# Two biases, one softmax sum and a block scaling written in another form, in a two-layer decoder kernel

## The chip, the cores and the metric

One core of a Trainium2 chip runs the whole program. The metric is the device time of one execution in microseconds. Engines are TensorE (PE, with its weight loads as PEld), VectorE (DVE), ScalarE (ACT), GpSimd (POOL) and SyncE (SP), which issues the DMAs. Each runs its own list of instructions in order, and they meet in semaphores.

## The reference

The input x is 8 items of 256 tokens by 512, with a context of 8 x 256 x 128. Two layers follow each other, each of three residual steps, every one on the layer norm of x:

```
layer 0   x += softmax(mask(q k' / sqrt(32))) v @ Wo.T + bo     16 heads of 32, causal;
                q = x Wq.T + bq, k = x Wk.T + bk, v = x Wv.T + bv
          x += softmax(q k' / 4) v      32 query heads of 16 on the context, 8 key heads, no mask
          x += mx(silu(mx(x, w_gate)) * mx(x, w_up), w_down)    512 -> 2048 -> 512
layer 1   x += ((scan + x Dp) * sigmoid(x Wg + bg)) @ Wo        h = exp(d A) h + d d, along the tokens
          x += causal attention of x on keys and values expanded from the context, 16 heads of 32
          x += x W.T + low-rank experts, 2 of 8 per token
```

`mx` rounds both operands in blocks of 32: a block is divided by a power of two taken from its largest absolute value, rounded to a few bits, and multiplied back.

## The kernel before, in words

`build` writes the instructions of every engine. Each stage is a class with one generator per engine, and each `yield` ends a piece. `TURNS0` holds, per engine, a long string of letters; `side_by_side` advances the generator that the next letter names. So the order on each engine is fixed, and the stages of neighbouring items are interleaved: in layer 0 the masked attention (`attn`, banks 0 to 2), the attention on the context (`mix`, banks 3 to 5), the rounding of the weights (`quantised`) and the hidden layer (`ffn`, banks 6 and 7); in layer 1 the scan (`ssm`), the attention on the context (`cross`) and the experts (`lora`). The program's item loop runs over 8 items, each with two blocks of 128 tokens (TT = 2) and four chunks of 128 features (DC = 4).

**Products.** Where fp32 exactness is wanted, an operand is a pair of fp16 tiles, high and low. `product` (its matmul stands on L200) makes three matmuls per pair. `Loader` brings a weight to a staging tile by DMA, copies it to the high half on ACT (L285) and subtracts on VectorE to get the low half (L292).

**`Attention`** is used twice, as `attn` and as `cross`. Per item: transpose the normed rows (L422), q and k for four chunks (L200, and for `attn` L431), v for two token blocks (L200), row maxima of the scores (L481 to L495 on TensorE, L679 and L683 on VectorE), then for each of 16 heads the transposed scores (L522, L523), an exponential on ACT into `p` (L642), and the causal mask on POOL (L737). A head's `p` is 128 x 384: first the key block 0 for all 256 queries, then key block 1 for queries 128 to 255. For every four heads, L534 makes the values' product in a column-tiled form (four matmuls side by side on 32 columns of the array each), and L542 the sums over keys. L542 keeps one row for each head and each query block, 32 rows of 128 columns for all 16 heads: `ones_of_four[:, 2c+t, :]` picks the row, and the three blocks of `p` are three matmuls of 128 columns per head. L692 takes the reciprocal of the 128 x 128 sums, L557 spreads it back over the features of a head (16 matmuls of 128 columns for each of two halves), L698 multiplies, L705 splits, and the output product (L200) follows; L719 adds it to x.

**The biases.** The value bias `bv` is not added to v, since the weights of a softmax sum to 1. Instead `bv @ Wo.T` is made once, with item 0's output product (12 matmuls on L200), added to x of item 0 (L713) and to the output bias `bo` (L715), which POOL adds to x for every item. The gate bias of the scan stage enters its bank by one matmul per token block (L1385), whose stationary `two_rows` has ones in row 0 and row 64, with the bias's high half in the upper and its low half in the lower rows of `g_b`.

**The rounding.** `dve_quantise` takes the blocks' maxima (L1133), clamps them (L1135), keeps the exponent as `e` (L1137), makes the inverse `inv` (L1139) and multiplies (L1142); `dve_rounded` clamps and multiplies back with `e` (L1148, L1150). It runs 5 times an item. `e` is larger than the block's scale by a constant factor; the factors WEIGHT, ROWS and GATE are carried through the products and taken out in the `Tanh` scale and, as DOWN, in the last addition to x (L1279, L1283). The 12 units of weights do the same (L794 to L822).

**Banks.** `Banks.take` makes TensorE wait until a PSUM bank has been read. Of several banks that wait on the same semaphore it issues one wait, with the larger value.

## Time and profile before

| | |
|---|---|
| time, median of 3 runs | 1603.94 us (1602.54, 1603.94, 1609.94) |
| the profiled execution: time, span | 1603.94 us, 1602.2 us |
| busy: TensorE, VectorE, ScalarE, GpSimd | 85%, 83%, 65%, 27% of the span |
| mean granted TensorE clock | 0.939 of full speed |
| last quantisation of layer 0, first gate bias of layer 1 | at 972 us, at 856 us (the layers overlap) |

The span runs from the first to the last instruction of the profile; the time holds the launch around it as well. Busy time is a sum over stages with different limits. The chain of work that ended last is followed back from the last instruction, at each step to what released it or to the instruction before it on its engine. A matmul on fp32 data appears as two records, and its length in the trace includes the way through the array, so that neighbours overlap; what a stream of them costs is read from start to start.

### The profile page before, as it was taken

How to read it: one execution, taken by the hardware profiler on the slowest of the kernel's cores; microseconds unless marked ns; L12 is line 12 of the kernel's file. 1: busy time of each engine (PE TensorE's matmuls, PEld its weight loads, DVE VectorE, ACT ScalarE, POOL GpSimd, SP SyncE). 2: the span in 40 equal slices, each digit the busy share in tenths (PEclk: the TensorE clock that was granted, in tenths of full speed). 3: DMA queues.
4: the chain of work that ended last, by engine and by line, in shares of the span. 5: the costliest groups of instructions: out<-in, count | busy, mean ns of one | idle time of the engine just before them, and what ended most of it. 6: DMA issues, size and time to landing. Idle time of an engine off the chain costs nothing.

```text
span 1602.2 us, 32850 instructions
## 1 busy us (share of the span) xinstructions
PE 1361.3 (85%) x13068; PEld 745.7 (47%) x13068; DVE 1332.5 (83%) x1965; ACT 1037.2 (65%) x1884; POOL 428.2 (27%) x495
## 2 busy tenths in 40 slices
PE   3778878879899999898978767879999998999986
PEld 2454535344445453444443333446555555555643
DVE  6988989979879888887798899888788888978743
ACT  3244365465673865765695769886899788989431
POOL 1432141132240422321331240241222313122310
PEclk9697989799999999999999988889999999999988
DMA  6313122200201111002120003011020211101020
GB/s 223 93 54 93 34 68 68 74 15 1 75 15 41 36 41 42 21 22 54 63 89 28 1 1 132 20 41 44 2 71 13 59 39 33 41 5 44 2 81 27
DMA packets 54201, 76.24 MB, mean 48 GB/s; under 512 B 8480, under 2 KB 23840, under 8 KB 53536
## 3 DMA queue, kind: packets, MB, share of 16 engines
q1 hardware_dynamic: 54048, 74.14, 16.2%
q8 instruction: 104, 1.70, 0.4%
q14 instruction: 49, 0.40, 0.1%
HBM read 38.98 MB, written 9.44 MB: 30 GB/s over the span
## 4 chain that ended last, share of the span: by engine, by line
PE 47%; DVE 29%; ACT 10%; issue 7%; POOL 4%; DMA 1%; SPq 1%; ACTq 0%; DVEq 0%; POOLq 0%
PE bank L200 16%; DVE mix_NM L1079 4%; PE bank L1178 4%; PE bank L534 3%; DVE ssm_HS L1537 2%; PE bank L542 2%; PE bank L522 2%; PE bank L992 2%; PE bank L1204 2%; PE bank L557 2%; DVE ffn_m L1133 2%; PE bank L977 2%; POOL attn_P L737 2%; PE bank L495 1%; DVE ffn_Z L1142 1%
## 5 line engine op out<-in xcount | busy, mean ns | idle before, releaser
L1052 ACT ACTIVATE mix_P<-bank 128x512 f32<-128x512 f32 x256 | 142.3, 604 | 50.6 <-PE bank L977 50.2
L1079 DVE TENSOR_REDUCE mix_NM<-bank 128x2 f32<-128x512 f32 x256 | 162.8, 682 | 11.2 <-PE bank L952 10.4
L737 POOL TENSOR_SCALAR_AFFINE_SELECT cross_P<-cross_P 128x256 f32<-128x256 f32 x128 | 90.5, 717 | 272.9 <-ACT cross_P L642 272.4
L1296 POOL TENSOR_TENSOR ffn_room<-ffn_room 128x512 f32<-128x512 f32 x64 | 89.9, 1406 | 263.9 <-ACT ffn_room L1235 167.0
L1537 DVE TENSOR_TENSOR_SCAN ssm_HS<-ssm_DA,ssm_DD 128x1024 f32<-128x1024 f32 x64 | 150.3, 2348 | 10.1 <-ACT ssm_DD L1488 5.5
L737 POOL TENSOR_SCALAR_AFFINE_SELECT attn_P<-attn_P 128x256 f32<-128x256 f32 x128 | 89.6, 713 | 243.7 <-ACT attn_P L642 243.7
L1485 ACT ACTIVATE ssm_DA<-ssm_Z,A_T 128x255 f32<-128x255 f32 x256 | 110.9, 498 | 3.1 <-DVE ssm_HS L1537 2.7
L642 ACT ACTIVATE attn_P<-bank 128x384 f32<-128x384 f32 x128 | 63.8, 498 | 63.1 <-PE bank L523 62.7
L642 ACT ACTIVATE cross_P<-bank 128x384 f32<-128x384 f32 x128 | 62.6, 489 | 50.9 <-PE bank L523 50.5
L1543 DVE TENSOR_TENSOR ssm_HS<-ssm_HS,ssm_CS 128x1024 f32<-128x1024 f32 x64 | 82.0, 1281 | 0.9
L1460 ACT ACTIVATE ssm_Z<-bank 128x512 f32<-128x512 f32 x128 | 72.2, 599 | 13.4 <-PE bank L1374 12.8
L1178 PE MATMUL bank<-gate,ffn_XQ 128*128 128x512 bf16 x256 | 68.8, 392 | 13.0 <-DVE ffn_room L1260 12.7
L992 PE MATMUL bank<-mix_P,mix_V 128*32 128x256 f32 x1024 | 69.6, 395 | 2.8 <-DVE mix_XN L1095 2.2
L1178 PE MATMUL bank<-up,ffn_XQ 128*128 128x512 bf16 x256 | 68.5, 392 | 0.5 <-ACT ffn_room L1235 0.5
L977 PE MATMUL bank<-mix_Q,mix_K 64*128 64x256 f16 x512 | 53.2, 288 | 18.3 <-ACT mix_P L1052 15.6
L1488 ACT ACTIVATE ssm_DD<-ssm_Z 128x1024 f32<-128x1024 f32 x64 | 67.2, 1050 | 0.0
L952 PE MATMUL bank<-mix_K,mix_Q 64*128 64x256 f16 x512 | 51.6, 281 | 16.6 <-DVE mix_NM L1079 15.1
L1204 PE MATMUL bank<-down,ffn_room 128*128 128x512 bf16 x256 | 64.9, 389 | 0.0
L1231 ACT ACTIVATE ffn_room<-bank 128x512 f32<-128x512 f32 x64 | 38.9, 607 | 34.3 <-PE bank L1178 34.1
L1260 DVE SCALAR_TENSOR_TENSOR ffn_room<-ffn_room,bank 128x512 f32<-128x512 f32 x64 | 43.5, 680 | 19.3 <-ACT ffn_room L1231 19.3
L522 PE MATMUL bank<-attn_stack 128*128 128x256 f16 x128 | 39.1, 305 | 21.9 <-ACT attn_P L642 16.6
L1150 DVE TENSOR_TENSOR ffn_room<-ffn_room,ffn_e 128x1024 bf16<-128x1024 bf16 x40 | 54.3, 1357 | 1.4
(410 smaller groups left out, 4043.3 us busy)
## 6 DMA issues: line engine op xcount, KB each, us to landing
attn_stack<-attn_P SPq DMA_DIRECT2D x96, 128.0 KB, 2.4
cross_stack<-cross_P SPq DMA_DIRECT2D x96, 128.0 KB, 2.4
ffn_room<-f_gate SPq DMA_DIRECT2D x4, 1024.0 KB, 5.3
XR<-x SPq DMA_DIRECT2D x8, 512.0 KB, 6.8
ffn_room<-f_up SPq DMA_DIRECT2D x4, 1024.0 KB, 5.6
ffn_room<-f_down SPq DMA_DIRECT2D x4, 1024.0 KB, 4.9
x_mid<-XR SPq DMA_DIRECT2D x8, 512.0 KB, 3.0
XR<-x_mid SPq DMA_DIRECT2D x8, 512.0 KB, 3.7
```

The lines of the kernel that those rows point to most:

```text
L200: last = nc.tensor.matmul(out, a_, b_, start=(start and i == 0), stop=(stop and i == len(terms) - 1))
L642: nc.scalar.activation(self.p[h % 8][:, :], bank[self.b[0]][:, 0:S + P], ACT.Exp, scale=HD1 ** -0.5).then_inc(self.p_ready, 1)
L737: nc.gpsimd.affine_select(out=diagonal, in_=diagonal, compare_op=ALU.is_ge, fill=0.0, base=0, pattern=[[0, 2], [1, P]], channel_multiplier ...
L977: last = nc.tensor.matmul(bank[b4[i]][:, k * S:(k + 1) * S], self.k[rows, v // 2, k * P:(k + 1) * P], self.q[rows, v, :], start=(k == 0), ...
L992: last = nc.tensor.matmul(bank[b][32 * j:32 * j + 32, half * S:(half + 1) * S], self.v[:, k, g, :], self.p[(4 * g + j) % 8][:, k * S:(k + ...
L1052: nc.scalar.activation(self.p[h % 8], bank[b4[h % 2]][:, :], ACT.Exp, scale=HD2 ** -0.5).then_inc(s["p_ready"], 1)
L1079: nc.vector.tensor_reduce(self.nm[:, t, 16 * i + 2 * g:16 * i + 2 * g + 2], bank[b4[u % 3]][:, :].rearrange("p (c k) -> p c k", c=2), AX.X ...
L1178: last = nc.tensor.matmul(bank[b][:, :], self.xq[:, k, T * P:(T + 1) * P], w[:, k, fb * 512:(fb + 1) * 512], start=(k == 0), stop=(k == DC ...
L1204: last = nc.tensor.matmul(bank[b][:, :], self.iqt[:, f, :], self.down16[:, f, :], start=(f == 0), stop=(f == FC - 1))
L1296: nc.gpsimd.tensor_tensor(self.inter[q % 2][:, 512 * (g % 2):512 * (g % 2) + 512], self.sg[g % 2], self.up[g % 2], ALU.mult).then_inc(s["i ...
L1485: nc.scalar.activation(self.da[:, G % 2, k, 1:S], self.z[:, h, 1:S], ACT.Exp, scale=self.A_T[:, h:h + 1])
L1537: nc.vector.tensor_tensor_scan(flat(self.hs), flat(self.da), flat(self.dd), 0.0, ALU.mult, ALU.add).then_inc(s["hs_ready"], 1)
```

## The change

Six edits:

1. The sums of the softmax keep one row per head over 256 queries, in two matmuls per head (256 and 128 columns) in place of three of 128. The reciprocal covers 256 columns in place of 128, and the spreading has 8 matmuls of 256 columns per half in place of 16 of 128. Fewer columns of `ones_of_four` are set at the start.
2. `bv` is added to v by two matmuls of 512 columns (high and low half against the identity) per token block. The product `bv @ Wo.T`, its two additions and the wait of POOL go. The Loader brings `bv` broadcast to 128 x 512 in place of 128 x 4, and the first value product waits for the fourth load in place of the third.
3. The gate bias enters by two such matmuls in place of one; `two_rows` and its three memsets go, and the low half is made over 128 rows in place of 64.
4. `dve_quantise` and the weights' rounding make a further small tile `sc`, the block scale without the constant factor (`e` times 16, 8 or 0.25), and multiply back with it; the factors leave `Tanh`, L1279 and L1283, which become plain additions.
5. `Banks.take` issues one wait per bank.
6. The counts that TensorE waits for (`done_pool`, `made`) follow the smaller number of constants.

```diff
     def take(self, *banks):
-        last = {}
         for b in banks:
             if b in self.reader:
-                signal, value = self.reader.pop(b)
-                last[signal.num] = (signal, max(value, last.get(signal.num, (signal, value))[1]))
-        for signal, value in last.values():
-            self.engine.wait_ge(signal, value)
+                self.engine.wait_ge(*self.reader.pop(b))
...
-        ones_of_four = sb(top, "ones_of_four", [P, 2 * DC, 32])
+        ones_of_four = sb(top, "ones_of_four", [P, DC, 32])
...
                     if n == self.first and t == 0 and self.bv is not None:
-                        pe.wait_ge(*self.weights.ready(3))
+                        pe.wait_ge(*self.weights.ready(4))
                     banks.take(b)
+                    if self.bv is not None:
+                        for i, part in enumerate((self.bv.high, self.bv.low)):
+                            nc.tensor.matmul(bank[b][:, :], identh[:], part[:, :], start=(i == 0), stop=False)
...
-                        for i, t in enumerate((0, 1, 1)):
+                        for k, part, first in ((0, slice(0, S), 0), (1, slice(S, S + P), P)):
                             for j in range(4):
-                                last = nc.tensor.matmul(bank[sums][32 * j:32 * j + 32, 0:P], ones_of_four[:, 2 * c + t, :],
-                                                        self.p[(4 * c + j) % 8][:, i * P:(i + 1) * P],
-                                                        start=(c == 0 and i == 0), stop=(c == DC - 1 and i == 2))
+                                last = nc.tensor.matmul(bank[sums][32 * j:32 * j + 32, first:S], ones_of_four[:, c, :],
+                                                        self.p[(4 * c + j) % 8][:, part], start=(c == 0 and k == 0),
+                                                        stop=(c == DC - 1 and k == 1))
...
-                    for i in range(2 * TT):
+                    for i in range(2):
                         for j in range(4):
-                            at = 32 * j + 2 * TT * half + i
-                            last = nc.tensor.matmul(bank[b][32 * j:32 * j + 32, i * P:(i + 1) * P],
-                                                    ident[:, at:at + 1].broadcast_to([P, HD1]), self.rc[:, 0:P],
+                            at = 32 * j + 2 * half + i
+                            last = nc.tensor.matmul(bank[b][32 * j:32 * j + 32, i * S:(i + 1) * S],
+                                                    ident[:, at:at + 1].broadcast_to([P, HD1]), self.rc[:, :],
                                                     start=True, stop=True)
...
-                        if n == self.first and c == 2 and t == 0 and self.bv is not None:
-                            banks.take(self.b[1])
-                            product(bank[self.b[1]][:, :], [
-                                (self.bv.view(lambda t_: t_[:, k:k + 1].broadcast_to([P, P])),
-                                 self.wo.view(lambda t_: t_[:, k, :])) for k in range(DC)]).then_inc(self.vo_ps, 1)
-                            banks.read_by(self.b[1], self.vo_done, 2)
...
-                nc.vector.reciprocal(self.rc[:, 0:P], bank[self.b[2]][:, 0:P]).then_inc(self.r_ready, 1)
+                nc.vector.reciprocal(self.rc[:, :], bank[self.b[2]][:, 0:S]).then_inc(self.r_ready, 1)
...
-                    if self.bv is not None and n == self.first and t == 0:
-                        dve.wait_ge(self.vo_ps, 1)
-                        nc.vector.tensor_tensor(x[:, :, :], x[:, :, :], broadcast(bank[self.b[1]][:, :], 1, TT), ALU.add
-                                                ).then_inc(self.vo_done, 1)
-                        nc.vector.tensor_tensor(self.bo[:, :], self.bo[:, :], bank[self.b[1]][:, :], ALU.add
-                                                ).then_inc(self.vo_done, 1)
-                        dve.wait_ge(self.vo_done, 2)
...
-                    if n == 1:
-                        pool.wait_ge(self.vo_done, 2)
...
+                scaled = own(nc.vector.tensor_scalar(q_sc, q_e, 0.25, None, ALU.mult))
...
+                own.wait(scaled)
...
-                nc.vector.scalar_tensor_tensor(blocks(self.w16), blocks(y), -6.0, broadcast(q_e, 2, BLOCK), ALU.max,
+                nc.vector.scalar_tensor_tensor(blocks(self.w16), blocks(y), -6.0, broadcast(q_sc, 2, BLOCK), ALU.max,
...
+                own(nc.vector.tensor_scalar(sc, e, back, None, ALU.mult))
                 own.wait()
                 nc.vector.tensor_tensor(blocks(self.z8[:, :]), blocks(src), broadcast(inv, 2, BLOCK), ALU.mult,
...
-                        nc.scalar.activation(self.sg[g % 2], bank[b4[0]][:, :], ACT.Tanh, scale=GATE / 2
+                        nc.scalar.activation(self.sg[g % 2], bank[b4[0]][:, :], ACT.Tanh, scale=0.5
...
-                nc.vector.scalar_tensor_tensor(x[:, 1, :], bank[b4[1]][:, :], DOWN, x[:, 1, :], ALU.mult, ALU.add
+                nc.vector.tensor_tensor(x[:, 1, :], x[:, 1, :], bank[b4[1]][:, :], ALU.add
...
-                            nc.tensor.matmul(bank[b][:, :], two_rows[:], self.g_b[:, :], start=True, stop=False)
+                            for i, part in enumerate((self.g_b.high, self.g_b.low)):
+                                nc.tensor.matmul(bank[b][:, :], identh[:], part[:, :], start=(i == 0), stop=False)
...
-                               + [(whole(bv), A["bv"]), (whole(wo), chunk(A["Wo"]))],
+                               + [(whole(bv), A["bv"].partition_broadcast(P)), (whole(wo), chunk(A["Wo"]))],
```

## Rows read from the trace of the kernel before

**Rows 1.** The page's busy times and chain by engine; the cores' clock.

```profile
PE 1361.3 (85%) x13068; PEld 745.7 (47%) x13068; DVE 1332.5 (83%) x1965; ACT 1037.2 (65%) x1884; POOL 428.2 (27%) x495
...
PE 47%; DVE 29%; ACT 10%; issue 7%; POOL 4%; DMA 1%; SPq 1%; ACTq 0%; DVEq 0%; POOLq 0%
...
core 0: 1602.2 us, clock 0.939
```

**Rows 2.** The chain by line, 120 to 800 us, then 800 to 1602.

```profile
by line: PE bank L200 10.2%; DVE mix_NM L1079 7.4%; PE bank L1178 7.0%; issue 7.0%; PE bank L992 4.3%; POOL attn_P L737 3.5%; PE bank L977 3.3%; PE bank L952 3.2%; PE bank L1204 3.1%; DVE ffn_m L1133 2.4%; PE bank L534 2.4%; DVE ffn_room L1
...
by line: PE bank L200 23.2%; issue 7.0%; DVE ssm_HS L1537 4.9%; PE bank L534 2.9%; DVE ssm_HS L1543 2.4%; PE bank L542 2.4%; POOL cross_P L737 2.2%; PE bank L1402 2.2%; PE bank L1374 2.1%; PE bank L522 2.1%; DVE mix_NM L1079 2.1%; PE bank L
```

**Rows 3.** Busy time of L200 on TensorE (instructions), clock, DMA, by stretch.

```profile
120.00:800.00 680.00, 149.85 (x915) 0.95 0.16 44
800.00:1602.00 802.00, 317.31 (x2016) 0.94 0.14 39
```

**Rows 4.** Groups on VectorE: busy us, mean ns; idle before, releaser.

```profile
L1133 DVE TENSOR_REDUCE ffn_m<-ffn_room 128x32 f32<-128x1024 f32 x40 | 48.4, 1210 | 2.0 <-ACT ffn_room L357 1.6
...
L1093 DVE RECIPROCAL mix_RS<-bank 128x16 f32<-128x16 f32 x32 | 8.1, 253 | 24.6 <-PE bank L1007 24.5
...
L692 DVE RECIPROCAL attn_RC<-bank 128x128 f32<-128x128 f32 x8 | 7.6, 955 | 12.4 <-PE bank L542 12.4
```

**Rows 5.** Timeline of TensorE, 240 to 248 us: start, length, records.

```profile
241.13 0.86 PE L534 MATMUL bank<-attn_P,attn_V 128*32 128x256 f32 x16 [0.93 <-POOL attn_P L737]
241.80 0.84 PE L542 MATMUL bank<-attn_P,ones_of_four 128*32 128x128 f32 x24
242.46 1.05 PE L992 MATMUL bank<-mix_P,mix_V 128*32 128x256 f32 x16
...
245.01 0.39 PE L977 MATMUL bank<-mix_Q,mix_K 64*128 64x256 f16 x4 [0.18 <-ACT mix_P L1052]
245.33 1.07 PE L992 MATMUL bank<-mix_P,mix_V 128*32 128x256 f32 x16
246.22 1.93 PE L557 MATMUL bank<-attn_RC,ident 128*32 128x128 f32 x64
```

**Rows 6.** Timeline around the first and the last of 16 reciprocals.

```profile
92.11 0.96 DVE L692 RECIPROCAL attn_RC<-bank 128x128 f32<-128x128 f32 x1 [5.96 <-PE bank L542]
...
93.13 1.95 PE L557 MATMUL bank<-attn_RC,ident 128*32 128x128 f32 x64 [1.08 <-DVE attn_RC L692]
...
1559.26 0.96 DVE L692 RECIPROCAL cross_RC<-bank 128x128 f32<-128x128 f32 x1 [1.53 <-PE bank L542]
...
1560.54 1.73 PE L557 MATMUL bank<-cross_RC,ident 128*32 128x128 f32 x55
```

**Rows 7.** Timeline of VectorE at 109.6 us.

```profile
109.64 0.17 DVE L344 TENSOR_SCALAR mix_negative<-mix_mv 128x2 f32<-128x2 f32 x1
109.72 0.16 DVE L345 TENSOR_SCALAR mix_var<-mix_mv 128x2 f32<-128x2 f32 x1
```

**Rows 8.** Timeline of TensorE at 600 us: two products of 512 columns.

```profile
600.76 0.38 PE L200 MATMUL bank<-l_wv_l,attn_XH 128*128 128x512 f16 x1
600.97 0.38 PE L200 MATMUL bank<-l_wv_h,attn_XL 128*128 128x512 f16 x1
```

**Rows 9.** Timeline at the first output product, and at the weights' split.

```profile
99.10 0.38 PE L200 MATMUL bank<-l_wo_h,l_bv_h 128*128 128x512 f16 x1
...
101.96 1.22 DVE L713 TENSOR_TENSOR XR<-XR,bank 128x1024 f32<-128x1024 f32 x1
...
103.90 1.28 DVE L719 TENSOR_TENSOR XR<-XR,bank 128x512 f32<-128x512 f32 x2
...
33.39 0.15 DVE L292 TENSOR_TENSOR l_bv_l<-attn_stack,l_bv_h 128x4 f16<-128x4 f32 x1
33.46 2.29 DVE L292 TENSOR_TENSOR l_wo_l<-attn_stack,l_wo_h 128x2048 f16<-128x2048 f32 x1
```

**Rows 10.** The chain in order of time, 96 to 104 us.

```profile
96.50 7.31 PE bank L200 x33
```

More of the change, by code:

```diff
@@ L228, in make_constants @@
             own.wait()
-            own(nc.gpsimd.memset(ones_of_four[:, 0, 1:2 * DC], 0.0))
-            for i in range(1, 2 * DC):
+            own(nc.gpsimd.memset(ones_of_four[:, 0, 1:DC], 0.0))
+            for i in range(1, DC):
                 own(nc.gpsimd.memset(ones_of_four[:, i, i:i + 1], 1.0))
@@ L290, in dve @@
                 dve.wait_ge(self.high_ready, self.first + i + 1)
-                rows = slice(P - w.low.shape[0], P)
-                nc.vector.tensor_tensor(w.low, self.staged(i)[rows], w.high[rows], ALU.subtract
-                                        ).then_inc(self.low_ready, 1)
+                nc.vector.tensor_tensor(w.low, self.staged(i), w.high, ALU.subtract).then_inc(self.low_ready, 1)
         def whole(w):
@@ L376, in __init__ @@
                 self.ql_ps = sem(f"{name}_ql_ps") if bq is not None else None
-                self.vo_ps, self.vo_done = ((sem(f"{name}_{part}") for part in ("vo_ps", "vo_done"))
-                                            if bv is not None else (None, None))
                 for_sems = lambda part: sem(f"{name}_{part}") if before is None else before.signals[part]
@@ L464, in pe @@
                                                         self.wv.view(lambda t_: t_[:, k, :]))],
-                                       start=(k == 0), stop=(k == steps - 1))
+                                       start=(self.bv is None and k == 0), stop=(k == steps - 1))
                     last.then_inc(self.v_ps, 1)
@@ L1128, in __init__, with dve_quantise @@
                 self.s = {part: sem(f"ffn_{part}") for part in names}
-            def dve_quantise(self, dve, own, src):
-                m, e, inv = (t_[:, :] for t_ in (self.m, self.e, self.inv))
+            def dve_quantise(self, dve, own, src, back):
+                m, e, inv, sc = (t_[:, :] for t_ in (self.m, self.e, self.inv, self.sc))
                 blocks = lambda t_: t_.rearrange("p (n b) -> p n b", b=BLOCK)
@@ L1149, in dve_rounded @@
                 own.wait()
-                nc.vector.tensor_tensor(blocks(dst), blocks(dst), broadcast(self.e[:, :], 2, BLOCK), ALU.mult
+                nc.vector.tensor_tensor(blocks(dst), blocks(dst), broadcast(self.sc[:, :], 2, BLOCK), ALU.mult
                                         ).then_inc(self.s["q_ready"], 1)
@@ L1272, in dve @@
                     dve.wait_ge(s["q_ready"], 5 * n + q + 1)
[L1273 removed]
+                    self.dve_quantise(dve, own, self.inter[q % 2], 8.0)
                     yield
@@ L1896, in make_columns @@
             pool.wait_ge(made, at + 1)
-            nc.gpsimd.memset(two_rows[:], 0.0).then_inc(made, 1)
-            for i in range(2):
-                pool.wait_ge(made, at + 2 + i)
-                nc.gpsimd.memset(two_rows[P // 2 * i:P // 2 * i + 1, :], 1.0).then_inc(made, 1)
-            pool.wait_ge(made, at + 4)
         def clear_cross(pool, n):
```

33 lines of the change are left out of this document (13 added, 20 removed).

## The prediction, written before the result was known

> **What bounds the kernel now.** I read the page first: busy shares and the chain of work that ended last, by engine. TensorE is busy 85% of the span and VectorE 83%, but the chain is 47% TensorE and 29% VectorE [rows 1]. No engine is the bound alone. The two hand the path back and forth, in an order that the program fixes. So work added to either reaches the end only where that engine holds the path. The question for each edit is therefore how many microseconds it adds, and what share of them arrives.
>
> For that share I set two views beside each other, by stage: the chain by line [rows 2], and the busy time of the same line [rows 3]. The split products at L200 hold 10.2% of the 680 us from 120 to 800, which is 69.4 us of the 149.85 us they are busy: 46%. From 800 on it is 23.2% of 802 us, 186 of 317.3 us: 59%. The reduction that opens a quantisation, L1133, holds 2.4% of 680 us, 16.3 us, of 27 x 1.21 us, which is what one takes [rows 4]: 50%. For VectorE as a whole I take 29% over 83%, 35%.
>
> The sum goes against the profiled execution, whose own time is 1603.94 us at a span of 1602.2 us. That is also the median of the three runs (1602.54 to 1609.94). A measurement here can hardly tell less than 0.5%, or 8.0 us, from no change: faster is below 1595.9, slower above 1612.0.
>
> **The change, part by part.**
>
> *Softmax sums.* The sums of a row block come as three matmuls of 128 columns per head now, and as one of 256 and one of 128 afterwards: 1536 columns for four heads either way. What does a record cost beyond its columns? At 241.13 to 242.46 the trace has both shapes in a row [rows 5]: L534, 16 records with 256 and 128 columns (the shape that L542 takes on), 0.67 us to the next start; L542, 24 records of 128, 0.66 us. The same columns, the same time. L557 halves its instructions and keeps 2048 columns per half: two halves last 1.95 us [rows 6]. Two groups of L992, each with 2048 columns in half as many records, need 0.89 us (start to next start) and 1.07 us (the whole of the last) [rows 5], 1.96 us. I take both at 0.
>
> *Reciprocal.* L692 goes from 128 to 256 elements per partition. It takes 955 ns for 128, and L1093 253 ns for 16 [rows 4], so 702/112 = 6.3 ns an element, and 128 more cost 0.80 us. The lowest price would be that of other operations, about 1.2 ns an element (L1133 takes 1210 ns for 1024), 0.15 us; the highest a plain doubling, 0.96 us. I take 0.80, the line through two sizes of the same operation: 16 x 0.80 = 12.9 us of VectorE. The Trainium skill (VectorE: DVE Perf Modes, "First, the fixed hardware budget") says that the reciprocal is an iterated divide with a repeat count of 8. At the page's 0.96 GHz that would be an estimated 8.3 ns an element, 1.07 us for 128 more and 17 us in all. The row speaks against so much, since the whole instruction takes 955 ns.
>
> What waits for it: L557 on TensorE, and whatever follows on VectorE. I compared the end of L692 with the start of L557 in all 16 cases; the first and the last stand in [rows 6]. In three (items 0 and 1 of the first attention, item 0 of the second) L557 starts within 0.06 us: 3 x 0.74 = 2.2 us arrive. The last item has 0.32 us to spare and nothing to fill it with: 0.5 us. Two more have 0.12 and 0.52 us, and lose 0.68 and 0.28, of which I take half, 0.5. Three have 0.8 us, seven 1.5 us or more. These ten delay only what follows on VectorE: 10 x 0.80 x 35% = 2.8, less because half of them have idle time behind them; I take 1.7. **Together 4.9 us.**
>
> *Quantisation.* One small tensor_scalar more in each of 40 quantisations and 12 weight units. It stands behind a neighbour with no wait between, as L345 behind L344, which starts 0.08 us after it [rows 7]; its own 0.17 us is the bound above, zero below. 40 x 0.08 x 50% = 1.6 us, and 12 x 0.1 x 50% = 0.6 us. **Together 2.2 us.** The plain add at L1279 and L1283 and the other constants of the scaling keep the same operands from the same places, so 0.
>
> *Bias matmuls.* Two of 512 columns for each of 16 row blocks in the first attention, 32 in all, and 16 more for the gate, where one already stands. Neighbours of this shape start 0.21 to 0.23 us apart at full clock [rows 8]; I take 0.217. Item 0 (4 matmuls) runs before 120 us, where the path is VectorE's, so 28 x 0.217 x 46% = 2.8 us, and 16 x 0.217 x 59% = 2.0 us. **Together 4.8 us.** Below: nothing, if TensorE's idle time takes them; above: all 48, 10.4 us, and double in a stretch at half clock.
>
> *What goes.* The product of the value bias with the output weights, 12 matmuls from 99.10 us, lies on the chain, inside one piece of 7.31 us of L200 [rows 10], and L713 and L715 follow it. VectorE is free at 101.96, but the first L719 starts at 103.90 [rows 9]. Without them TensorE ends 12 x 0.217 = 2.6 us sooner, and L719 can start at 101.96: **minus 1.9 us**, once. The wait on POOL for item 1 goes too; POOL is busy 27% of the span [rows 1] and gains nothing that the end would see.
>
> *Loading.* L292 for the value bias grows from 4 to 512 elements, on the chain at 33.4 us, where VectorE is packed; the next L292 takes 2.29 us for 2048 elements [rows 9], so 1.1 ns an element, 0.5 us. The broadcast load, the larger copy on ACT and the later count that the first value product waits for lie ahead of a wait for all weights, and cost nothing unless the 256 KB land late. The gate bias's two halves have as many elements per partition as before. **Plus 0.5 us.** POOL makes fewer constants at the start, hidden behind the first loads; 0.
>
> *Waits.* Taking two banks of the mixing stage now issues two waits where one stood, about 256 times, on TensorE, ahead of the scores and products of mixing. The nearest evidence is L977 to L992: half of those units wait on one semaphore and half on two, and where the data is there at full clock nearly all of them start 0.32 us after L977 does, as at 245.01 [rows 5]. A second satisfied wait shows nothing. Where TensorE really waits, the second wait names the later event of the same semaphore, the very one it waits for today. 0, with 0.05 us each (12.8 us) as the bound above.
>
> Sum: 4.9 + 2.2 + 4.8 - 1.9 + 0.5 = **10.5 us**. A path that is just short of the longest takes over once it is pushed, which the shares leave out, so I round up: 1603.9 + 11 = 1615 us.
>
> **The rivals.**
> *Absorbed.* Only what stands on the zero-slack path arrives: reciprocals 2.2 + 0.5, half of the quantisations 1, bias 1 to 2, minus 1.9 and plus 0.5, so 2 to 5 us: 1606 to 1609. For it: each addition is small, and TensorE is idle for 15% of the span. Against it: the path passes through just these lines.
> *Nothing absorbed.* Both engines hold each other up, and every microsecond arrives: 12.9 + 4.4 + 10.4 - 1.9 + 0.5 = 26 us, 1630. For it: the fixed order lets no engine run ahead. Against it: 83% and 85% busy leave gaps.
> *Fewer instructions make it faster.* 512 matmuls, 1024 records, go from L542 and L557. If each dropped record freed its whole spacing, 0.66/24 = 27 ns [rows 5], that is 28 us, and the time 1604 - 28 + 10.5 = 1586. It decides (below 1595.9) from 18 ns a record. Against it stands the equality in [rows 5]. The Trainium skill (TensorEngine Tiling (Array Packing), "Instruction Overhead") gives each matmul about 60 cycles of overhead. By that rule the estimate would be 512 x 25 ns = 12.8 us off, and a time near 1602, no change.
> *The clock.* The first L557 already has 1.08 us of idle TensorE ahead of it [rows 6]. If a longer wait brings another stretch to the 1.2 GHz level, each 10 us of it costs up to 5. I keep this inside the range.
>
> **How the numbers follow.** Forecast (1609 to 1621) 0.55; absorbed 0.22; nothing absorbed (1621 to 1632) 0.17; fewer instructions 0.06. Four fifths of the forecast lies above 1612: slower 0.44 + 0.17 = 0.61. Same: 0.11 + 0.22 + half of the last = 0.36. Faster 0.03. The range is 1605 to 1627: it leaves out the upper half of nothing absorbed, the last rival and the forecast's own tails, some 0.17.
>
> **What would show it.** L692 at 1.76 us for 256 elements; 40 more small VectorE instructions 0.08 us apart; L542 with 16 records in 0.66 us; L557 in 1.95 us for two halves; 48 new 512-column matmuls at 0.217 us; L719 of item 0 where L713 stands now; L977 to L992 still 0.32 us. The prediction is wrong if TensorE's waits for the reciprocal grow by far more or less than 3 us, if the two-wait units start later, if the granted clock (mean 0.939 [rows 1]) moves by over 0.01, or if L542 gets shorter by 0.1 us or more a group.

## The result

The kernel after takes 1617.74 us (median of 4 runs, 1616.75 to 1620.45), the kernel before 1604.54 us on the same chip (4 runs, 1602.54 to 1609.94). The ratio is 1.0085, 95% interval [1.0063, 1.0106]: 13.2 us slower by the medians, 10 to 17 by the interval, where 11 were forecast, and inside the range of 1605 to 1627.

The page of the kernel after (span of the profiled execution, busy times, the chain by engine and by line), and its clock:

```profile
span 1615.7 us, 31163 instructions
...
PE 1374.8 (85%) x12080; PEld 729.4 (45%) x12080; DVE 1347.9 (83%) x2015; ACT 1038.7 (64%) x1884; POOL 423.9 (26%) x488
...
PE 48%; DVE 29%; ACT 10%; issue 7%; POOL 3%; DMA 1%; SPq 0%; ACTq 0%; DVEq 0%; POOLq 0%
PE bank L193 17%; DVE mix_NM L1058 4%; PE bank L1158 4%; PE bank L526 3%; PE bank L534 2%; PE bank L514 2%; DVE ssm_HS L1518 2%; PE bank L971 2%; DVE ffn_m L1112 2%; PE bank L487 2%; DVE ffn_Z L1122 2%; PE bank L549 2%; PE bank L931 2%; PE bank L956 2%; DVE ffn_room L1130 1%
...
core 0: 1615.7 us, clock 0.937
```

Beside [rows 1], the shares are the same, 48% and 29% of the chain for TensorE and VectorE. VectorE has 15.4 us more of work, TensorE 13.5 us more. The clock is 0.937 for 0.939. The loss does not come from one place, but it is not even either. I compared the starts of the 16 reciprocals in the two traces (times are those of before). The kernel after is behind by 1.6 us at 92 us, ahead by 1.4 at 167 and by 0.2 at 243, then behind by 2.0 at 341, 5.4 at 561, 8.1 at 781, 6.7 at 1080, 11.1 at 1143, 11.6 at 1212 and 11.5 at 1559; the span ends 13.5 us later. So nearly 10 us come between 167 and 781 us, in layer 0, and nothing comes between 1212 and 1559, although five longer reciprocals and half of the added matmuls of the gate bias lie there. The step at 1080 to 1143 is looked at under the clock, below.

The reciprocal and the spreading that waits for it, by group (busy, mean ns; idle before, releaser):

```profile
L678 DVE RECIPROCAL cross_RC<-bank 128x256 f32<-128x256 f32 x8 | 14.1, 1758 | 7.6 <-PE bank L534 7.6
L678 DVE RECIPROCAL attn_RC<-bank 128x256 f32<-128x256 f32 x8 | 14.0, 1754 | 12.9 <-PE bank L534 12.9
...
L549 PE MATMUL bank<-attn_RC,ident 128*32 128x256 f32 x256 | 16.1, 383 | 4.3 <-DVE attn_RC L678 4.3
...
L549 PE MATMUL bank<-cross_RC,ident 128*32 128x256 f32 x256 | 15.5, 382 | 2.1 <-DVE cross_RC L678 2.1
```

The reciprocal takes 1754 to 1758 ns, 0.80 us more than in [rows 4]. TensorE's idle time ahead of the spreading is 4.3 + 2.1 us; in the trace of before the same two groups show 2.2 + 0.5. The timeline around the first and the last reciprocal, which answers to [rows 6]:

```profile
93.75 1.76 DVE L678 RECIPROCAL attn_RC<-bank 128x256 f32<-128x256 f32 x1 [6.82 <-PE bank L534]
...
95.56 1.72 PE L549 MATMUL bank<-attn_RC,ident 128*32 128x256 f32 x28 [1.88 <-DVE attn_RC L678]
...
1570.75 1.76 DVE L678 RECIPROCAL cross_RC<-bank 128x256 f32<-128x256 f32 x1 [1.53 <-PE bank L534]
...
1572.56 1.93 PE L549 MATMUL bank<-cross_RC,ident 128*32 128x256 f32 x32 [0.47 <-DVE cross_RC L678]
```

The timeline of TensorE that answers to [rows 5]:

```profile
240.92 0.86 PE L526 MATMUL bank<-attn_P,attn_V 128*32 128x256 f32 x16
241.59 0.83 PE L534 MATMUL bank<-attn_P,ones_of_four 128*32 128x256 f32 x16
242.24 1.05 PE L971 MATMUL bank<-mix_P,mix_V 128*32 128x256 f32 x16
...
244.88 0.39 PE L956 MATMUL bank<-mix_Q,mix_K 64*128 64x256 f16 x4 [0.27 <-ACT mix_P L1031]
245.21 1.07 PE L971 MATMUL bank<-mix_P,mix_V 128*32 128x256 f32 x16
246.10 1.91 PE L549 MATMUL bank<-attn_RC,ident 128*32 128x256 f32 x32
```

The sums (L534) now take 16 records and 0.65 us to the next start (0.66 before). The two halves of L549 take 1.91 us for 1.95. The scores at 244.88 are followed by L971 0.33 us later (0.32 before).

The small operation added to a quantisation, between its neighbours:

```profile
371.29 0.18 DVE L1118 TENSOR_SCALAR ffn_inv<-ffn_e 128x32 int32<-128x32 int32 x1
371.38 0.17 DVE L1120 TENSOR_SCALAR ffn_sc<-ffn_e 128x32 f32<-128x32 f32 x1
371.59 1.22 DVE L1122 TENSOR_TENSOR ffn_Z<-ffn_room,ffn_inv 128x1024 fp8e4<-128x1024 f32 x1
```

L1120 starts 0.09 us after L1118. Over all 40 quantisations the median from L1118 to L1122 is 301 ns; from L1139 to L1142, its counterpart, it was 217. So 84 ns each.

The first output product's addition to x, the two bias matmuls of a row block, and then the chain's piece at the first output product, which answers to [rows 10]:

```profile
103.12 1.23 DVE L789 TENSOR_SCALAR ffn_room<-ffn_room 128x2048 f32<-128x2048 f32 x1
...
104.27 1.28 DVE L698 TENSOR_TENSOR XR<-XR,bank 128x512 f32<-128x512 f32 x2
...
606.05 0.39 PE L451 MATMUL bank<-l_bv_h,identh 128*128 128x512 f16 x1
606.27 0.38 PE L451 MATMUL bank<-l_bv_l,identh 128*128 128x512 f16 x1
```

```profile
98.91 5.14 PE bank L193 x23
```

The bias matmuls start 0.22 us apart. The piece is 5.14 us long, 23 records, for 7.31 us and 33. The first L698 starts at 104.27. The first reciprocal began 1.64 us later than in [rows 6] and took 0.80 us longer, so without the removal it would have been 103.90 + 2.44 = 106.34: by this reckoning 2.1 us won, where 1.9 were forecast.

### The profile page after: what moved, and what is told of

Its sections match the earlier page's. It is cut to its first block, busy times and chain, and to the rows that moved or that the text cites. A ratio compares the mean times of both kernels' runs of the same rounds, so it can differ in the third digit from the quotient of the medians.

```text
span 1615.7 us, 31163 instructions
## 1 busy us (share of the span) xinstructions
PE 1374.8 (85%) x12080; PEld 729.4 (45%) x12080; DVE 1347.9 (83%) x2015; ACT 1038.7 (64%) x1884; POOL 423.9 (26%) x488
## 4 chain that ended last, share of the span: by engine, by line
PE 48%; DVE 29%; ACT 10%; issue 7%; POOL 3%; DMA 1%; SPq 0%; ACTq 0%; DVEq 0%; POOLq 0%
PE bank L193 17%; DVE mix_NM L1058 4%; PE bank L1158 4%; PE bank L526 3%; PE bank L534 2%; PE bank L514 2%; DVE ssm_HS L1518 2%; PE bank L971 2%; DVE ffn_m L1112 2%; PE bank L487 2%; DVE ffn_Z L1122 2%; PE bank L549 2%; PE bank L931 2%; PE bank L956 2%; DVE ffn_room L1130 1%
## 5 line engine op out<-in xcount | busy, mean ns | idle before, releaser
L1058 DVE TENSOR_REDUCE mix_NM<-bank 128x2 f32<-128x512 f32 x256 | 164.4, 683 | 10.5 <-PE bank L931 9.8
L714 POOL TENSOR_SCALAR_AFFINE_SELECT attn_P<-attn_P 128x256 f32<-128x256 f32 x128 | 86.3, 686 | 247.0 <-ACT attn_P L628 246.9
L1441 ACT ACTIVATE ssm_Z<-bank 128x512 f32<-128x512 f32 x128 | 72.2, 598 | 13.6 <-PE bank L1354 12.9
L971 PE MATMUL bank<-mix_P,mix_V 128*32 128x256 f32 x1024 | 69.0, 392 | 3.0 <-DVE mix_XN L1074 2.5
L1130 DVE TENSOR_TENSOR ffn_room<-ffn_room,ffn_sc 128x1024 bf16<-128x1024 bf16 x40 | 53.7, 1342 | 1.4
```

Of the source, the lines that this page charges most:

```text
L714: nc.gpsimd.affine_select(out=diagonal, in_=diagonal, compare_op=ALU.is_ge, fill=0.0, base=0, pattern=[[0, 2], [1, P]], channel_multiplier ...
L971: last = nc.tensor.matmul(bank[b][32 * j:32 * j + 32, half * S:(half + 1) * S], self.v[:, k, g, :], self.p[(4 * g + j) % 8][:, k * S:(k + ...
L1058: nc.vector.tensor_reduce(self.nm[:, t, 16 * i + 2 * g:16 * i + 2 * g + 2], bank[b4[u % 3]][:, :].rearrange("p (c k) -> p c k", c=2), AX.X ...
```

## The experiments

The experiments fall into three sets, each on a chip of its own and each with its own executions of the kernel before: the four p_ runs (35 executions of before, median 1607.3 us), then w_rev, u_waits, r_x3 and s_64 (24, 1607.0 us), then r_256, r_64, u_sums and f_order (35, 1608.0 us). The ratio given with a comparison is not exactly the quotient of its medians. The microseconds behind the colon are the ratio times 1607, those in brackets its bounds. A comparison of this kind is uncertain by 2 to 4 us, which is the size of many effects here, so the traces carry much of the weight.

The mean granted clock of each execution was measured too, and it matters for effects of this size. The executions of the kernel before lie between 0.930 and 0.945 of full speed, with a mean of 0.936 in each set, and within each set a clock lower by 0.001 goes with a time longer by 1.0 to 1.1 us.

### One edit at a time

**p_sums: the first edit alone** (sums, reciprocal over 256, spreading).

> The kernel before with the first edit alone: sums over 256 columns, reciprocal of 256 elements, spreading by 256 columns. By the prediction's step this brings 4.9 us (16 reciprocals of 0.80 us more, of which 38% arrive; matmuls free): 1609. The rival in which fewer instructions free TensorE expects a time below before, by up to 28 us. The rival in which nothing is absorbed expects 12.9 us: 1617. L542 should keep 0.66 us a group, the reciprocal should take 1.76 us.

1611.0 us, ratio 1.0025 [1.0003, 1.0047]: +4.0 us (0.5 to 8). The forecast of 4.9 lies inside; nothing absorbed (12.9) and a gain lie outside.

**p_bias: edits 2 and 3 alone** (both biases).

> The kernel before with the two bias edits alone (48 more matmuls of 512 columns, the one product of value bias and output weights and its two additions gone, a longer split at the start). The prediction's steps: 4.8 - 1.9 + 0.5 = 3.4 us: 1608. Nothing absorbed: 10.4 - 1.4 = 9.0 us: 1613.5. Absorbed: 0 us or slightly less than before.

1609.8 us, 1.0009 [0.9987, 1.0031]: +1.5 us (-2 to 5). Less than the 3.4 forecast, within what can be told. But its 12 executions ran at a mean clock of 0.9397, the 35 of before at 0.9361, a difference of nearly three standard errors. By the 1.07 us for 0.001 in this set, I estimate that the same edits at equal clock would cost about 5 us.

**p_scale: edit 4 alone** (the further scale tile).

> The kernel before with the rounding edit alone (52 more small instructions on VectorE). The prediction's step: 2.2 us: 1606.5. Nothing absorbed: 4.4 us: 1609. Each new instruction should start 0.08 us after L1139's and move its next neighbour by about as much.

1610.7 us, 1.0021 [0.9997, 1.0045]: +3.4 us (-0.5 to 7). In agreement with 2.2, and with 0 and 4.4 as well.

**p_waits: edit 5 alone** (one wait per bank).

> The kernel before with one wait per bank in place of one per semaphore, and nothing else. The prediction's step: 0 us, within 2 us of before. The rival: 0.05 us for each of 256 waits, 12.8 us if all arrive, about 6 at the shares used. The start of L992 after L977 should stay at 0.32 us.

1612.2 us, 1.0028 [1.0006, 1.0050]: +4.5 us (1 to 8). The expectation of nothing, within 2 us, has failed by the middle value; the interval reaches down into it. The four parts make 4.0 + 1.5 + 3.4 + 4.5 = 13.4 us, as much as the whole. That they meet so closely is luck: each is uncertain by 3.5 us, and they share one set of executions of before, so the sum is uncertain by more than 7.

### What a second wait costs

In the kernel before, a mixing unit whose scores wait for the two exponentials of the unit before. The first lines are the timeline (start, length); the last is the instructions of TensorE's sequencer that do nothing but wait (count, then ns min/median/max):

```profile
213.04 1.08 ACT L1052 ACTIVATE mix_P<-bank 128x512 f32<-128x512 f32 x2 [0.17 <-PE bank L977]
...
214.18 0.13 PEld L977 LDWEIGHTS bank<-mix_Q,mix_K 64*128 64x128 f16 x4 [1.66 <-ACT mix_P L1052]
...
L123 PEldq EVENT_SEMAPHORE  x538: 51/51/51, 45.8 to 1586.2; - x180
```

The exponential ends at 214.12 and the weight load starts at 214.18. The same place with edit 5 alone:

```profile
217.27 1.09 ACT L1048 ACTIVATE mix_P<-bank 128x512 f32<-128x512 f32 x2 [0.17 <-PE bank L973]
...
218.47 0.16 PEld L973 LDWEIGHTS bank<-mix_Q,mix_K 64*128 64x128 f16 x4 [1.72 <-ACT mix_P L1048]
...
L119 PEldq EVENT_SEMAPHORE  x786: 51/51/51, 46.3 to 1597.4; - x197
```

The exponential ends at 218.36 and the weight load starts at 218.47, 0.11 us behind. Over all such starts the median is 51 ns before and 113 with the edit, and 54 and 115 for the other unit of mixing (L952 of before, behind the maxima). What stands between is a wait-only instruction: it starts 37 ns after the exponential's end and lasts 51 ns, and the weight load starts 25 ns behind it. The weight load itself carries a wait on the same semaphore in both traces; before, it is the only one. There are 786 such instructions for 538.

This says where it counts. When the data is there, TensorE's sequencer is ahead and the instruction is hidden, as the forecast saw in [rows 5]. When TensorE stands waiting, it is not. I counted, in the traces, the starts of a weight load out of over 0.1 us of idle time with such an instruction ending 10 to 45 ns before: 103 in the kernel before, 191 in this one. (With other bounds the counts move, and the difference stays at 87 to 95.) 88 x 61 ns = 5.4 us of later weight loads, and 4.5 arrived. In some of these places an earlier matmul still ran; where it had ended over 0.1 us before as well, there are 62 and 119, which makes 3.5 us.

**w_rev: one wait per bank, in the reverse order.** The forecast had claimed that the second wait names the very event that was waited for anyway. That is so; what may matter is the order. If the wait that is issued first rides on the weight load itself and later ones become instructions ahead of it, then issuing the last event's wait first must bring 51 ns back with as many waits.

```diff
     def take(self, *banks):
-        for b in banks:
+        for b in reversed(banks):
             if b in self.reader:
                 self.engine.wait_ge(*self.reader.pop(b))
```

> Like p_waits (one wait per bank), but the two waits of a pair in the other order: the bank that comes free last first. Seen in p_waits: where TensorE stands waiting, L973 starts 113 ns after the exponential's end in place of 51 ns, and a semaphore record lies between. Theory: of two waits the one issued first rides on the matmul, the second becomes an instruction of its own ahead of it, so that the last event is met by that instruction and the matmul has to be taken up after it, 61 ns. Then this order brings 51 ns back, and the time of the kernel before, within 0.3%. Rival: any second wait costs 61 ns, wherever the last event is met: 113 ns here too, and the time of p_waits, about 4 us over before.

1609.1 us, 1.0003 [0.9988, 1.0019]: +0.5 us (-2 to 3).

```profile
210.09 1.09 ACT L1048 ACTIVATE mix_P<-bank 128x512 f32<-128x512 f32 x2 [0.17 <-PE bank L973]
...
211.23 0.13 PEld L973 LDWEIGHTS bank<-mix_Q,mix_K 64*128 64x128 f16 x4 [1.66 <-ACT mix_P L1048]
...
L119 PEldq EVENT_SEMAPHORE  x786: 51/51/51, 45.7 to 1592.7; - x197
```

Again 786 wait-only instructions, and yet the weight load starts at 211.23, 0.05 us after the exponential's end at 211.18; the medians are 51 and 53 ns. 118 starts have such an instruction just ahead. So what delays the start is not the number of waits but which of them is met last, and the rival in which any second wait costs 61 ns is out. The trace shows this. The times agree with it (+0.5 against +4.5 us), but their difference of 4.0 us is itself uncertain by 4.3, and would not carry it alone.

**u_waits: the kernel after with edit 5 undone.**

> The changed kernel with the merged waits of the kernel before (this part alone undone). If p_waits's 0.28% were the waits and not chance, it takes back 3 to 5 us: 1613.5 against 1617.7. If that was chance: 1617.7. The start of mixing's matmuls after the exponential should be back at 51 ns from 113.

1619.0 us (7 runs), 1.0060 [1.0039, 1.0082]. The delay is back at 51 ns and the count at 103. The ratio is lower than that of the whole (1.0085) by 0.25%, 4 us, as p_waits alone says; the two intervals overlap, so this run by itself does not show it. The time of 1613.5 expected if the waits cost 3 to 5 us was not reached: the median is 1619.0, and the agreement is one of ratios.

**f_order: mending the kernel before.** The count of 103 names places where the kernel before pays the 61 ns: L1178 (the bank's wait comes last and is issued second), L1007 and L1633 (the same event is waited for twice).

```diff
-                    pe.wait_ge(s["xqt_ready"], TT * n + T + 1)
                     for w, b in ((self.gate16, bg_), (self.up16, bu)):
...
                         banks.take(b)
+                        if b == bg_:
+                            pe.wait_ge(s["xqt_ready"], TT * n + T + 1)
...
-                        pe.wait_ge(s["ot_ready"], C + 1)
                         banks.take(b)
...
-                pe.wait_ge(s["hw_ready"], n + 1)
                 banks.take(b)
```

> The kernel before, with two kinds of waits of TensorE mended: a wait that is issued twice for the same event (ahead of the mixing's transposes, L1002, and of the experts' transpose, L1630) is issued once, and ahead of the gate's product the wait for the bank, which comes last, is issued first. In the trace of before, 17, 14 and 3 starts out of idle time have a semaphore instruction just ahead at these places (L1178, L1007, L1633): 34 x 61 ns = 2.1 us, of which by the run with one wait per bank some eight tenths arrive: -1.7 us, ratio 0.999. If the waits' order is worth nothing, 1.000. The difference is hardly more than a comparison can tell, so the trace decides: starts after idle with such an instruction ahead go from 103 to about 70.

1607.6 us against 1608.0, 0.9997 [0.9983, 1.0012].

```profile
L123 PEldq EVENT_SEMAPHORE  x434: 51/51/51, 45.3 to 1587.9; - x145
```

The count of delayed starts fell from 103 to 67, as it should, and wait-only instructions at this line from 538 to 434. A gain of 1.7 us fits the interval, and so does none. It is the same speed as far as a comparison can tell, and no version here that computes the same result beats the kernel before.

### The reciprocal and the shapes of the matmuls

**r_256: the kernel before with only the reciprocal made wide.** Its second half is computed and not used.

```diff
-                nc.vector.reciprocal(self.rc[:, 0:P], bank[self.b[2]][:, 0:P]).then_inc(self.r_ready, 1)
+                nc.vector.reciprocal(self.rc[:, 0:S], bank[self.b[2]][:, 0:S]).then_inc(self.r_ready, 1)
```

> The kernel before, with only the reciprocal over 256 columns in place of 128 (the second half is computed and not used). Matmuls as before. The first edit alone gave +4.0 us. If the reciprocal is all of that: 1754 ns an item, and +4 to +5 us (ratio 1.0025 to 1.003). If the wider, fewer matmuls took part: they cost something, and this run comes out below +3; or they give something back, and it comes out above +6.

1612.6 us, 1.0025 [1.0011, 1.0040]: +4.0 us (2 to 6), the same ratio as the whole first edit. The reciprocal and the spreading by group:

```profile
L692 DVE RECIPROCAL attn_RC<-bank 128x256 f32<-128x256 f32 x8 | 14.0, 1755 | 15.1 <-PE bank L542 15.1
...
L557 PE MATMUL bank<-attn_RC,ident 128*32 128x128 f32 x512 | 17.7, 291 | 4.3 <-DVE attn_RC L692 4.3
...
L557 PE MATMUL bank<-cross_RC,ident 128*32 128x128 f32 x512 | 15.6, 274 | 2.1 <-DVE cross_RC L692 2.1
```

TensorE waits 4.3 + 2.1 us, as in the kernel after. So the first edit's cost is the reciprocal's, and its 512 fewer matmuls give nothing that can be seen, with an error of some 4 us.

**r_64: the reciprocal over 64 columns**, each used for two blocks of queries. The second half of a block's queries is scaled by the sums of the first.

```diff
-                            last = nc.tensor.matmul(bank[b][32 * j:32 * j + 32, i * P:(i + 1) * P],
-                                                    ident[:, at:at + 1].broadcast_to([P, HD1]), self.rc[:, 0:P],
+                            last = nc.tensor.matmul(bank[b][32 * j:32 * j + 32, i * P:(i + 1) * P].rearrange("p (a k) -> p a k", a=2),
+                                                    ident[:, at:at + 1].broadcast_to([P, HD1]), broadcast(self.rc[:, 0:64], 1, 2),
...
-                nc.vector.reciprocal(self.rc[:, 0:P], bank[self.b[2]][:, 0:P]).then_inc(self.r_ready, 1)
+                nc.vector.reciprocal(self.rc[:, 0:64], bank[self.b[2]][:, 0:64]).then_inc(self.r_ready, 1)
```

> The kernel before, with the reciprocal over 64 columns, each used twice in the spreading (so the second half of a block's queries gets the scale of the first: that part of the computation is wrong). Matmuls as before. The reciprocal should take 0.55 us, 0.40 less, 6.4 us of VectorE. If delays and gains of this size arrive by the same third: -2 us (0.9985 to 0.999). If a shorter reciprocal brings nothing, 0. If it is as the run with blocks of 64, +4.6 us, something in the shorter reciprocal would be the cause; the theory is that it lies in that run's matmuls, so it should not be.

1606.7 us against 1608.0, 0.9984 [0.9968, 1.0000]: -2.6 us (-5 to 0).

```profile
L692 DVE RECIPROCAL attn_RC<-bank 128x64 f32<-128x64 f32 x8 | 4.4, 555 | 11.4 <-PE bank L542 11.4
...
L557 PE MATMUL bank<-attn_RC,ident 128*32 128x128 f32 x512 | 16.2, 274 | 1.4 <-DVE attn_RC L692 1.4
L557 PE MATMUL bank<-cross_RC,ident 128*32 128x128 f32 x512 | 15.6, 274 | 0.1
```

**r_x3: the reciprocal of before made three times in a row.**

```diff
-                            banks.read_by(sums, self.r_ready, n + 1)
+                            banks.read_by(sums, self.r_ready, 3 * n + 3)
...
-                    pe.wait_ge(self.r_ready, n + 1)
+                    pe.wait_ge(self.r_ready, 3 * n + 3)
...
-                nc.vector.reciprocal(self.rc[:, 0:P], bank[self.b[2]][:, 0:P]).then_inc(self.r_ready, 1)
+                for i in range(3):
+                    last = nc.vector.reciprocal(self.rc[:, 0:P], bank[self.b[2]][:, 0:P])
+                    last.then_inc(self.r_ready, 1)
+                    if i < 2:
+                        dve.wait_ge(self.r_ready, 3 * n + i + 1)
```

> The kernel before with each reciprocal of 128 elements made three times, which adds no matmul and changes none: 16 x 2 x 0.95 = 30 us more on VectorE, and L557 later by 1.9 us in every item. By the shares used for 0.80 us (38% arrive) 11.5 us; since only 7 of the 16 have 1.5 us or more to spare, more of it should arrive here: 12 to 20 us, so 1616 to 1624. Nothing absorbed: 1634. If the reciprocal were off the path: below 1609.

1636.6 us (4 runs), 1.0175 [1.0151, 1.0199]: +28 us (24 to 32). More than any expectation but the one with nothing absorbed.

```profile
L693 DVE RECIPROCAL attn_RC<-bank 128x128 f32<-128x128 f32 x24 | 22.9, 956 | 11.1 <-PE bank L542 10.5
...
L557 PE MATMUL bank<-attn_RC,ident 128*32 128x128 f32 x512 | 17.1, 284 | 9.0 <-DVE attn_RC L693 9.0
L557 PE MATMUL bank<-cross_RC,ident 128*32 128x128 f32 x512 | 16.5, 283 | 8.5 <-DVE cross_RC L693 8.3
```

Take the three runs together. Per item the reciprocal is 0.40 us shorter, 0.80 longer, and 2 x 0.956 = 1.91 longer, which is 6.4, 12.9 and 30.6 us of VectorE over 16 items. At the end -2.6, +4.0 and +28 us arrive: about 40% (0 to 80), 31% (14 to 50) and 92% (79 to over 100). The long delay arrives in full or nearly so; the two short ones can't be told from each other. TensorE's idle time ahead of the spreading, 2.7 us in the kernel before, is 1.5, 6.4 and 17.5: changes of -1.2, +3.7 and +14.8. The forecast's list of slack explains these numbers, item by item. From the end of L692 to the start of L557 the trace of before has 0.06 us three times (nothing to spare), then 0.12, 0.32, 0.52, 0.79, 0.80, 0.80, 1.49, 1.60, 1.83, 2.46, 2.56, 2.92 and 2.95. A delay of 0.80 us exceeds these by 3.7 us in all, one of 1.91 us by 14.5; TensorE's idle time grew by 3.7 and 14.8. Of the 28 us about half is thus TensorE waiting here. The other half is open. The four executions of r_x3 have a mean clock of 0.9313, those of before 0.9363, which by the 1.04 us for 0.001 of this set goes with an estimated 5 us; whether the longer waits lowered the clock was not tested. The rest may come by way of what follows on VectorE; no run took it apart.

**s_64: sums in blocks of 64 queries**: twice the matmuls in L542 and L557 (here L541 and L556) with the same columns, and a reciprocal over 64.

```diff
-                        for i, t in enumerate((0, 1, 1)):
+                        for i, t in enumerate((0, 1, 2, 3, 2, 3)):
...
-                                last = nc.tensor.matmul(bank[sums][32 * j:32 * j + 32, 0:P], ones_of_four[:, 2 * c + t, :],
+                                last = nc.tensor.matmul(bank[sums][32 * j:32 * j + 32, 0:64], one_at_15[:, 15 - 4 * c - t:47 - 4 * c - t],
...
-                    for i in range(2 * TT):
+                    for i in range(8):
...
```

> The first edit the other way: sums and reciprocal in four query blocks of 64 in place of two of 128. 64 elements take 0.95 - 64 x 6.3 ns = 0.55 us, 0.40 us less, 16 times: minus 6.4 us of VectorE, of which 38% would arrive, minus 2.4 us: 1602. TensorE has the same columns in 48 records a group in place of 24, and 128 in place of 64 for the spreading. If a record is free, L542 stays at 0.66 us and the spreading at 1.95; if each costs about 25 ns at least, 48 records last 1.2 us, 64 x 0.55 + 16 x 1.3 = 56 us more of TensorE, and the time is 1620 to 1660.

1611.6 us, 1.0029 [1.0014, 1.0043]: +4.6 us, neither the -2.4 nor the 1620 and more. With r_64 beside it, which has the same reciprocal and comes out at -2.6, the matmuls of 64 columns cost 0.0029 + 0.0016 = 0.45%, 7 us (4 to 11), for 1280 more of them. In the trace a group of 48 records takes 786 ns to the next start for 771, and two halves of the spreading 1926 for 1885: 64 x 15 + 16 x 41 ns = 1.6 us. Ahead of L556, the spreading, TensorE is idle for 3.7 us in all where r_64 has 1.5, and for 2.2 of them the profile shows nothing that it waits for. The rest of the 7 us was not found.

**u_sums: the kernel after with the first edit undone.**

> The kernel after with the first edit undone (sums, reciprocal and spreading as before). The parts add up if this takes 4 us off the kernel after: ratio to before 1.006, 1613.6 us. If the reciprocal hurts more once the other edits have used up the slack: 6 us or more off, ratio 1.0045 or less.

1612.5 us, 1.0022 [1.0008, 1.0036]. Undoing the first edit takes 0.63% off (1.0085 to 1.0022), 10 us, where the edit alone adds 4. The errors of the two differences are about 0.25% and 0.2%, so their intervals still overlap. One could read a rising price into it, as if a delay cost more where the other edits have used up the slack. The clock offers a simpler reading: the 12 executions of u_sums have a mean clock of 0.9405, seven executions of the kernel after 0.9369. By the 1.05 us for 0.001 this goes with an estimated 4 of the 10 us, and the 6 left agree with 4.0. TensorE's idle time ahead of the spreading also falls by 3.7 us (6.4 to 2.7), as much as the edit alone adds. Whether the edit itself moves the clock is open. The parts add up as far as these runs can tell.

## Why the prediction came out right, point by point

The time is right with one step wrong and others mis-sized: the waits, put at nothing, measured +4.5 us. That the total lies 2 us from the forecast is partly luck.

- **Reciprocal, +4.9: right in price and mechanism, and in size as far as can be told.** 1.76 us as forecast. Three sizes now lie on the line: 555, 956 and 1756 ns for 64, 128 and 256 elements, 6.3 ns each. By the Trainium skill (VectorE: DVE Perf Modes, "First, the fixed hardware budget") the estimate was 8.3 ns an element, 1.07 us for 128 more; the trace has 0.80. TensorE's waits grew by 3.7 us; the forecast's parts for them were 2.2 + 0.5 + 0.5, and it called itself wrong if they grew by far more or less than 3. What arrived is 4.0 (2 to 6 in r_256) of 4.9, so the 1.7 for VectorE's path was too much, if anything.
- **Sums and spreading at 0: right.** The groups are 5 and 19 ns shorter in the median (766 for 771, 1866 for 1885), 0.6 us in all, and r_256 without them has the ratio of p_sums with them. The rival of fewer instructions wanted 18 ns a record. By the Trainium skill (TensorEngine Tiling (Array Packing), "Instruction Overhead") 60 cycles a matmul made an estimated 12.8 us for 512 of them. The comparison of p_sums with r_256 excludes that here (0.00%, with an error of some 0.26%, 4 us). s_64 shows that the rule is not empty in the other direction: 7 us for 1280 matmuls of 64 columns is 5 to 6 ns each, still far from 25.
- **Quantisation, +2.2.** 84 ns each, for 80 forecast. Alone it measured 3.4 (-0.5 to 7), which contains 2.2, but also nothing and all of it: the share of 50% that arrives stays unproven.
- **Bias matmuls, +4.8, removal -1.9, loading +0.5.** The spacing of 0.22 us is as forecast, and the value bias's L284 took 687 ns for the 155 of before, the 0.5. Alone the two biases measured 1.5, for a sum of 3.4; the interval holds both, and at equal clock it would be about 5. So the size of these terms stays open in both directions. Two shares look wrong in single traces. The removal seems worth more than 1.9: from the first reciprocal to the second the four traces with the bias edits (after, p_bias, u_waits, u_sums) gain 3 to 4 us on before, two of them in spite of a reciprocal 0.80 us longer, while p_sums, p_scale, p_waits, w_rev and f_order lie between a gain of 1.9 and a loss of 1.5. And the 59% for the gate's matmuls isn't seen where half of them stand, at 1212 to 1559 us: p_bias loses nothing there (4.2 us behind at 1212, 3.2 at 1559).
- **Waits, 0: wrong.** This is the step that failed. The argument "where TensorE really waits, the second wait names the later event of the same semaphore, the very one it waits for today" is true and misses the point: the wait for the last event used to ride on the weight load and is now an instruction of its own between the event and the weight load. It costs 61 ns a time, at 88 places, and +4.5 us (1 to 8). By the forecast's own list this was a sign of being wrong ("if the two-wait units start later"), and it came true: 113 ns after the event for 51. The bound above that the forecast set (0.05 us each, 12.8 us) had nearly the right price for one; it was left at 0 since the only units looked at were those whose data was there, and those do still start after 0.32 us.
- **Sum 10.5, rounded up to 11.** Measured one by one the terms are 4.0 + 1.5 + 3.4 + 4.5 = 13.4, for 4.9 + 3.4 + 2.2 + 0. By these middle values, reciprocal and biases, 2.8 us too high together, covered more than half of the 4.5 that the waits lacked. Each is uncertain by 3.5 us, and at equal clock the biases would not be too high, so which terms made up for the waits is not shown.
- **The clock.** Granted clock by stretch, for before and then after (busy and count of PE, PEld, DVE, ACT, POOL; PEclk; DMA share; GB/s):

```profile
core 0: us, PE busy (x) PEld busy (x) DVE busy (x) ACT busy (x) POOL busy (x), PEclk, DMA share, GB/s
54.00:92.00 38.00, 25.72 (x263) 14.73 (x263) 31.77 (x33) 11.97 (x24) 14.38 (x18) 0.60 0.37 114
1100.00:1190.00 90.00, 83.26 (x844) 50.34 (x843) 72.24 (x141) 69.75 (x125) 18.57 (x27) 1.00 0.21 51
```

```profile
54.00:92.00 38.00, 25.93 (x209) 12.82 (x208) 32.58 (x34) 10.82 (x22) 13.86 (x16) 0.55 0.39 119
1108.00:1198.00 90.00, 83.92 (x749) 48.87 (x747) 69.51 (x128) 66.31 (x118) 17.29 (x25) 0.94 0.21 51
```

In the two profiled executions the mean moved by 0.002, well under the 0.01 named, and the other executions say the same: 0.9369 over seven of the kernel after, 0.936 over the 94 of before in the three sets. But it moved in places: 0.60 to 0.55 at 54 to 92 us, and 1.00 to 0.94 at 1108 to 1198, where the kernel after has 10 us at the 1.2 GHz level that the profiled execution of before has not. Most of the step from 6.7 to 11.1 us behind stands there. Stretches like it are in the profiled executions of r_256, r_64 and f_order as well, and single executions of one kernel differ by 10 us and more (before: 1598 to 1615), so I take this stretch for scatter. The edits themselves are not all neutral: the biases alone go with a clock higher by 0.0036 (standard error 0.0013), the waits alone with one lower by 0.0015 (0.0011). No run tested why.

## What to carry to other kernels

Of several waits ahead of an instruction, issue the one that is met last first: on TensorE it then rides on the instruction, and the other, met earlier, cost nothing that could be told here (w_rev, -2 to 3 us). In two engines that take turns, price a delay against the list of slacks, item by item, and not with one share: here about a third of 0.8 us arrived, and nine tenths of 1.9. Beside a difference of a few microseconds put the granted clocks of the executions, since they can differ by as much. A sum that comes out right proves none of its terms; only the edits run one by one, with their traces, showed that a zero among them was some 4.5 us.

## What the runs showed of the hardware

- A wait-only instruction of TensorE lasts 51 ns. Where the data is there it doesn't show (0.32 us from L977 to L992 with one wait and with two). Between an event and a weight load that stands waiting for it, it moves the start from 51 to 113 ns after the event (p_waits); with the two waits in the other order the start is at 51 again (w_rev).
- Column-tiled fp32 matmuls on 128 x 32 tiles: for equal columns, 16 records of 256 and 128 columns take as long as 24 of 128 (766 and 771 ns to the next start), and 48 of 64 hardly longer (786). Yet the kernel with those of 64 was about 7 us (4 to 11) slower, of which 1.6 us stand in these groups and 2.2 in idle time ahead of the spreading; the rest is open.
- The reciprocal costs 6.3 ns an element per partition at 64, 128 and 256 elements, with some 155 ns beside.
- Of one kernel, executions with a granted clock lower by 0.001 were longer by 1.0 to 1.1 us (94 executions of the kernel before, 0.930 to 0.945).
